# Mixture-of-experts block: gates spread over partitions once a chunk, products weighted six steps later, gate computation placed between steps

## The reference, cut to what matters

```
def _L1_ffn_ref(x, w_gate, w_g, w_u, w_d):      # 8 experts, 2 chosen, 176 hidden units each
    scores = x @ w_gate
    topk_scores, topk_idx = top_k(scores, 2)
    topk_probs = softmax(topk_scores)
    gating = sum(one_hot(topk_idx, 8) * topk_probs[..., None], axis=-2)
    hidden = silu(einsum('bsd,edm->ebsm', x, w_g)) * einsum('bsd,edm->ebsm', x, w_u)
    expert_out = einsum('ebsm,emd->ebsd', hidden, w_d)
    return einsum('bse,ebsd->bsd', gating, expert_out)
...
x = x + 0.5 * _L1_ffn_ref(layernorm(x), ...)    # twice in the program
```

## Time and profile before

| | |
|---|---|
| three timed executions | 3160.64, 3164.51, 3164.62 us; median 3164.51 |
| profiled execution, its own time | 3132.56 us |
| its span, first to last instruction | 3130.8 us |
| PE / DVE / ACT / POOL busy, share of the span | 80 / 82 / 72 / 64 % |
| mean granted PE clock, 1.00 = 2.4 GHz | 0.931 |
| first call of `ffn1`: start, first matmul of step 0, end | 944.3, 962.2, 1170.65 us |
| second call of `ffn1`: the same | 2903.7, 2921.6, 3127.7 us |

### The profile page before, as it was taken

One profiled execution on the slowest core, in us unless ns is written; L12 is line 12 of the kernel. 1 busy time (PEld: TensorE's weight loads), 2 busy tenths in 40 slices (PEclk: granted clock), 3 DMA queues, 4 the chain that ended last, 5 costly groups with the idle time before them and its releaser, 6 DMA issues. The chain is left out here.

```text
span 3130.8 us, 61223 instructions
## 1 busy us (share of the span) xinstructions
PE 2497.2 (80%) x18663; PEld 1032.7 (33%) x18790; DVE 2578.9 (82%) x4251; ACT 2257.5 (72%) x2453; POOL 1995.7 (64%) x1350
## 2 busy tenths in 40 slices
PE   3655999997658984788888888888888888874899
PEld 3632333334654552122222222222222222213455
DVE  4666888885566656899999999999999999977665
ACT  4432777776444543599999999999999999992454
POOL 4510222222634441699999999999999999983444
PEclk9976999998778996799999999999999999995899
DMA  3222100010210002000000000000000000000000
GB/s 114 68 74 71 30 28 29 28 29 8 64 51 1 1 0 88 14 15 12 12 13 14 12 12 14 13 12 12 14 13 12 12 15 12 12 1 1 4 11 14
DMA packets 77234, 74.71 MB, mean 24 GB/s; under 512 B 16112, under 2 KB 57592, under 8 KB 76992
## 3 DMA queue, kind: packets, MB, share of 16 engines
q1 hardware_dynamic: 72832, 64.47, 7.0%
q0 software_dynamic: 4288, 8.82, 0.9%
HBM read 48.04 MB, written 24.42 MB: 23 GB/s over the span
## 5 line engine op out<-in xcount | busy, mean ns | idle before, releaser
L1730 POOL TENSOR_TENSOR a_sg<-a_sg,a_shifted 128x1664 f32<-128x1664 f32 x256 | 955.6, 3733 | 21.4
L1927 DVE TENSOR_REDUCE a_mx<-a_pm 128x1 f32<-128x1024 f32 x512 | 619.4, 1210 | 21.9 <-PE a_pm L1769 21.8
L1936 DVE TENSOR_SCALAR a_sg<-a_pa 128x1024 int32<-128x1024 int32 x512 | 619.2, 1209 | 4.2 <-PE a_pa L1769 3.9
L1849 ACT ACTIVATE a_pt<-a_pb 128x1024 f32<-128x1024 f32 x512 | 523.6, 1023 | 108.4 <-PE a_pb L1769 108.4
L1786 PE MATMUL a_po<-a_pt,a_Vh 128*32 128x512 f32 x2048 | 540.6, 607 | 2.2 <-ACT a_sg L1868 2.2
L1786 PE MATMUL a_po<-a_sg,a_Vh 128*32 128x512 f32 x2048 | 540.6, 607 | 0.0
L1727 POOL TENSOR_SCALAR a_shifted<-a_sg,a_parh 128x1664 f32<-128x1664 f32 x256 | 470.4, 1838 | 101.9 <-DVE a_sg L1936 64.2
L1864 ACT ACTIVATE a_sg<-a_sg,a_parh 128x2048 f32<-128x2048 f32 x256 | 511.9, 2000 | 0.0
L1868 ACT ACTIVATE a_sg<-a_sg 128x2048 f32<-128x2048 f32 x256 | 489.9, 1914 | 0.0
L1769 PE MATMUL a_pm<-all_K,all_Q 96*128 96x512 bf16 x1024 | 316.2, 391 | 149.9 <-DVE a_mx L1927 123.8
L1548 ACT ACTIVATE a_pt<-a_ring 128x1024 f32<-128x1024 f32 (+2 forms) x384 | 313.5, 846 | 167.4 <-PE a_ring L1475 164.1
(11 more groups left out here) (278 smaller groups left out, 4718.6 us busy)
## 6 DMA issues: line engine op xcount, KB each, us to landing
all_Q<-q_parts SPq DMA_DIRECT2D x256, 48.0 KB
all_K<-k_parts SPq DMA_DIRECT2D x256, 48.0 KB
k_parts<-p_parts SPq DMA_DIRECT2D x16, 384.0 KB, 2.8
all_Q<-a_rows SPq DMA_DIRECT2D x384, 2.0 KB
e_recs<-routed_rows SPq DMA_DIRECT2D x70, 64.5 KB, 1.8
n_xn<-expert_rows SPq DMA_DIRECT2D x16, 256.0 KB, 4.9
q_parts<-p_parts SPq DMA_DIRECT2D x16, 192.0 KB, 2.3
q_parts<-p_parts SPq DMA_DIRECT2D x8, 384.0 KB, 2.6
```

The source lines that it names most:

```text
L1730: nc.gpsimd.tensor_tensor(buf[:, :, 0:CUT], buf[:, :, 0:CUT], shifted[:], ALU.mult)\
L1849: nc.scalar.activation(pt[(j - LT) % 4][:, i, :], pb[:], ACT.Exp, scale=SC)\
L1927: nc.vector.tensor_reduce(mx[:, (j // PER) % 2, t:t + 1], pm[:], AX.X, ALU.max)\
L1936: nc.vector.tensor_scalar(sg[(j - LS) % 4][:, i, :].bitcast(I32), pa[:].bitcast(I32), SIGN_OFF, None, ALU.bitwise_and).then_inc(abs_done, 1)
```

## The change

The hidden units are laid out anew: of each tile's 128 partitions, 16 belong to each expert. So one and the same spread of gates over partitions serves all 11 tiles of a chunk. In detail:

- The `sel` matrix, its load, `gateT`, `gate3`, the bf16 identity, the three-way split of the gates, the 32 transposes ahead of the steps and the seventh matmul of every step go.
- POOL makes `wide` (`widen`), the gates of four token tiles with each expert's value repeated 16 times, once a chunk. PE transposes it (`turn`, 4 fp32 transposes a chunk) into `psm`, after step k=5 of the chunk.
- DVE's `products` is split in `product` (`su`) and `weigh` (`hid`). `weigh` for a step is issued six steps later, `high` and `low` seven steps later. `su` grows from 2 to 11 tiles, and PE no longer waits for `hid`.
- The output of a chunk is cut in four pieces, one token tile (33 matmuls) each, issued after steps k=9 of the next chunk and k=1, 4 and 6 of the one after it. `psy` takes two banks used in turn; DVE adds each piece one step later. The last seven pieces come after the last step.
- The gate computation is cut in three parts of DVE's stream, ahead of products 0, 1 and 4 of chunk 0. The Exp moves behind the third silu on ACT.

The diff, cut to its core:

```diff
-    sel = m.sb("sel", [96, KT1, P], BF16)
-        eng.dma_start(sel[:], w["sel"].rearrange("r (k p) -> r k p", p=P)).then_inc(sem, 16)
...
+    LAG = 6
+    TURN = 5
+    PIECES = ((1, 2, 1), (4, 2, 2), (6, 2, 3), (9, 1, 0))
...
+        wide = m.sb("wide", [P, 2, 4, E1, P // E1])
-        psy = m.ps("psy", [P, 4, D])
+        psy = m.ps("psy", [P, 2, CH])
...
-                nc.gpsimd.memset(gate3[:], 0.0).then_inc(cleared, 1)
+                def widen(c, p):
+                    if known(c, 1):
+                        pool.wait_ge(gate_ready, 1)
+                    elif not known(c, 2):
+                        pool.wait_ge(turned, c - 1)
+                    nc.gpsimd.tensor_copy(wide[:, p], gate[:, bass.ds(4 * c, 4), :].unsqueeze(3)
+                                          .broadcast_to([P, 4, E1, P // E1])).then_inc(widened, 1)
...
+                def turn(c, p):
+                    pe.wait_ge(widened, c + 1)
+                    if not known(c, 2):
+                        pe.wait_ge(hid_done, KT1 * (c - 1))
+                    for q in range(4):
+                        last = nc.tensor.transpose(psm[:, p, q * P:(q + 1) * P],
+                                                   wide[:, p, q].rearrange("p e i -> p (e i)"), ident[:])
+                    last.then_inc(turned, 1)
...
                         pe.wait_ge(silu_done, s - 1)
                         pe.wait_ge(su_done, s - 1)
-                        pe.wait_ge(hid_done, s - 1)
...
-                    nc.tensor.matmul(psm[:, b, :], sel[:, k, :], gateT[:, bass.ds(c * CH, CH)],
-                                     start=True, stop=True).then_inc(m_done, 1)
...
+                def output(c, p, q):
+                    if q == 0:
+                        pe.wait_ge(low_done, KT1 * c + KT1)
+                    if not known(4 * c + q, 2):
+                        pe.wait_ge(added, 4 * c + q - (1 if isinstance(c, int) or q != 1 else 0))
+                    for k in range(KT1):
...
+                def body(c, p):
+                    live = not after(c)
+                    for k in range(KT1):
+                        if live:
+                            step(c, p, k)
+                            if k == TURN:
+                                turn(c, p)
+                        for at_k, back, q in PIECES:
+                            if at_k == k and not known(c, back):
+                                if live or back == 2:
+                                    output(c - back, (p + back) % 2, q)
+                    if not live:
+                        for q in range(4):
+                            output(c - 1, 1 - p, q)
...
+                def weigh(c, p, k):
+                    s = KT1 * c + k
+                    if k == 0:
+                        dve.wait_ge(turned, c + 1)
                     dve.wait_ge(su_done, s + 1)
-                    if s_min(s) >= 3:
+                    if not known(s, 3):
                         dve.wait_ge(low_done, s - 2)
-                    nc.vector.tensor_tensor(hid[:, k % 4, :], psm[:, b, :], su[:, b, :], ALU.mult)\
+                    nc.vector.tensor_tensor(hid[:, k % 4, :], psm[:, p, :], su[k], ALU.mult)\
                         .then_inc(hid_done, 1)
...
+                        if known(c, 1):
+                            gates(k)
+                        if live:
+                            product(c, p, k)
+                        then = earlier(c, p, k, LAG)
+                        if then:
+                            weigh(*then)
```

More of the change, by code:

```diff
@@ L760, in ffn1, with slots @@
         psm = m.ps("psm", [P, 2, CH])
-        psy = m.ps("psy", [P, 4, D])
[L762 to L768, removed]
+        psy = m.ps("psy", [P, 2, CH])
+        chain, e2, saved, widened, gate_ready, turned = (
+            m.sem(x) for x in ("chain", "e2", "saved", "widened", "gate", "turned"))
+        g_done, u_done, silu_done, su_done, hid_done, high_done, low_done, y_done, added = (
+            m.sem(x) for x in ("gd", "ud", "silu", "sud", "hidd", "high", "low", "yd", "added"))
+        def slots(eng, body):
             for p in range(2):
@@ L840, in step @@
                         nc.tensor.matmul(out[:, b, :], low, xh, start=False, stop=True).then_inc(done, 1)
-                    nc.tensor.matmul(psm[:, b, :], sel[:, k, :], gateT[:, bass.ds(c * CH, CH)],
-                                     start=True, stop=True).then_inc(m_done, 1)
[L844 to L854, removed]
+                def output(c, p, q):
[4 more added lines that the diff above has]
+                    for k in range(KT1):
+                        high, low = (part[p][:, k, q * P:(q + 1) * P] for part in (hidh, hidl))
+                        nc.tensor.matmul(psy[:, q % 2, 0:D], high, wdh[:, k, :], start=(k == 0), stop=False)
+                        nc.tensor.matmul(psy[:, q % 2, 0:D], high, wdl[:, k, :], start=False, stop=False)
+                        last = nc.tensor.matmul(psy[:, q % 2, 0:D], low, wdh[:, k, :], start=False,
+                                                stop=(k == KT1 - 1))
@@ L855, in output, with body @@
                     last.then_inc(y_done, 1)
-                def chunk(c, p):
+                def body(c, p):
+                    live = not after(c)
                     for k in range(KT1):
[L859 to L864, removed]
+                        if live:
[9 more added lines that the diff above has]
+                            output(c - 1, 1 - p, q)
@@ L866, in _ @@
+                slots(pe, body)
             @block.scalar
             def _(act):
[L868 to L873, removed]
                 def silu(c, p, k):
@@ L891, in chunk @@
                     for k in range(KT1):
[L892 to L899, removed]
+                        if live:
+                            silu(c, p, k)
+                        if known(c, 1) and k == 2:
+                            act.wait_ge(e2, 1)
+                            nc.scalar.activation(pr[:, 1, :], pr[:, 0, :], ACT.Exp).then_inc(e2, 1)
@@ L908, in _ @@
[L908 to L915, removed]
@@ L943, in products @@
                         .then_inc(hid_done, 1)
-                def add(c):
-                    dve.wait_ge(y_done, c + 1)
-                    for q in range(4):
-                        nc.vector.scalar_tensor_tensor(X[:, 4 * c + q, :], psy[:, q, :], 1.0 / WSCALE,
-                                                       X[:, 4 * c + q, :], ALU.mult, ALU.add).then_inc(added, 1)
-                def chunk(c, p):
-                    for k in range(KT1):
-                        products(c, p, k)
-                        if k == EARLY - 1 and not (isinstance(c, int) and c == 0):
-                            add(c - 1)
```

127 lines of the change are left out of this document (71 added, 56 removed).

## The result

| | before | changed |
|---|---|---|
| median of the timed runs | 3162.57 us (3160.55 to 3164.62, 4 runs) | 3089.99 us (3088.97 to 3090.72, 4 runs) |
| ratio | | 0.9781, 95% interval 0.9769 to 0.9793 |
| profiled execution, span | 3132.56, 3130.8 us | 3088.97, 3086.9 us |
| first call of `ffn1`, start to end | 226.3 us | 189.2 us |
| second call | 224.0 us | 189.7 us |

The kernel is 72.6 us faster; 60 were predicted. The two calls, read in one profile of each kernel, account for 37.1 + 34.3 = 71.4 us. The two profiled spans differ by only 43.9 us, because the profiled execution of the kernel before was an unusually quick one ahead of the change's place; the first experiment shows this.

A forecast was written before the change was run, and what follows sets the result against it. PE's matmuls plus a two-step wait for `hid` were taken as the bound; calls change by -31.1 and -28.7 us, the start by -0.5, so 3164.5 - 60.3 = 3104 us, range 3092 to 3113.

The forecast's parts named there:

- the fourteen steps: Step 6 of chunk 0 to step 9 of chunk 1: DVE sets the pace, 1.46 us a step, 20.4 us.
- What bounds the steps: Kernel before: seven matmuls take 1.51 us a step, but waiting for `hid` makes two steps take 3.17 us.
- The front: Before a call's first step: step 0 no longer waits for gates, first matmul from 17.8 to about 0.1 us, -17.7 us.
- The first steps: Chunk 0 up to step 6, at half clock: step 6 starts 14.2 us in; gates between steps cost 3.6 us.
- The table loads: ACT's switches to Exp and back: 1.28 us a load, no drain; with the skill's drain, 5.5 us longer.
- the rival built on it: DVE sets the pace everywhere: a chunk costs 23.9 us, 18 us more in all, 3122; chance 0.13.
- Six chunks at 22.45 us: The six full chunks of a call: PE's stream of 22.05 us plus 0.4 each, 134.7 us.
- handover: Full chunks: 0.05 us added for each of eight changes a chunk between steps, turn and pieces.
- The tail: After a call's last step: PE idles 5.4 us, clock falls, 21.4 us; +7.0 and +9.6 us for the calls.
- At the start: Kernel start: one DMA issue goes from a queue that is waited for, -0.5 us.
- POOL's copies: POOL's 512-element copy, once a chunk: 0.7 us, no cost to DVE; rival that it makes the kernel slower, chance 0.02.
- The profiled execution: Whole kernel: the timed median's 32 us above the profiled execution, not located in the trace, was taken as unchanged.

The follow-up runs named there:

- the first experiment: The unchanged kernel before, profiled once more; one run, 3158.69 us.
- the later wait: Against the kernel before, PE's wait for `hid` of step s-2 moved from ahead of a step's first matmul to ahead of its seventh; 3148.05 us, ratio 0.9959.
- the changed kernel's second profile: The changed kernel run once more, unaltered, on the same chip as the version with the last output summed tile by tile; 3093.02 us, ratio 0.9778.

## Why the prediction was right, and where it was off

The mechanism was the forecast one in every part but the fourteen steps below, and the gain was larger than forecast. The measured 3090 lies 2 us below the forecast's own range of 3092 to 3113, an outcome that had a chance of 0.04. The base accounts for 2 us: the prediction started from 3164.5, and the median beside the result is 3162.6.

- **What bounds the steps.** PE's stream plus a two-step wait for `hid`. Both held: the later wait gave 13 us, and a seventh matmul in each step of the changed kernel cost 34 to 36.
- **The front, -17.7.** Measured -17.8: the first matmul starts with the call.
- **The first steps, 14.2 us to step 6.** Measured 13.0 and 14.4. The two calls differ by when the clock rose, 3.1 and 6.0 us after the first matmul; 4.9 was taken. PE's two pauses are where they were expected, for product 1 and for the copy. The copy was put at 0.7 and took 0.61.
- **The table loads.** Silu 2 ended at 977.43, the load began at 977.44 and Exp 1.29 us later; the next load began 0.02 after Exp's end, and silu 1.29 after that. The drain of about 1.38 us that the Trainium skill adds ("ScalarE: Activation LUTs", "What ACT_TABLE_LOAD costs") does not show. The prediction's estimate from it, 5.5 us more in all, would have made 3110, the worse number.
- **Fourteen steps without outputs, 20.4 us. This step failed.** They took 18.7 and 18.6, at 1.29 to 1.30 a step and 0.5 for the turn of chunk 1. The prediction read DVE's pace as 0.73 us an instruction off rows in which the product's start was set by PE and the weighting's by the product just ahead of it. Ready instructions of this size start 0.60 apart, so DVE needs 1.20 to 1.30 a step and not 1.46, and PE sets the pace here too. With every weighting twice, three instructions took 1.80. The distance of two instructions of which one waits is not the engine's pace. The size was off by 3.5 us over both calls, and the rival built on it was no rival.
- **Six chunks at 22.45 us.** Measured 22.05, PE's sum to the hundredth. The 0.05 us a handover, 4.8 us in all, was an allowance for nothing; the earlier trace rows had shown none.
- **The tail, 21.4 us in both calls.** Measured 20.4 and 19.4, 3 us less. POOL's low parts went at 1.12 us rather than 1.19 and ended 10.0 us after the last step, not 10.9. PE idled 3.67 us and not 5.4, for this reason and because the wait of 0.65 us for an add came before. The clock fell to half in both calls, as taken, but in the second only 3.3 us of output ran at half, against 5.3 in the first, and that call's output took 1.0 us less.
- **At the start, -0.5 us,** is too small to be seen here.
- **Sum.** Start 1, fourteen steps 3.5, handovers 4.8, tail 3.0: these make up the 12 us between 60 and 72. All of them err to the dear side, so nothing cancelled.
- **POOL's copies.** Eight in a call at 0.61 us, and the products and weightings beside them took their usual 0.68 to 0.69. By the Trainium skill ("GPSIMD Engine Reference", "Specifications") POOL contends with DVE instructions in a two-port mode or with two SBUF inputs. These have one input in PSUM, and the trace agrees.
- **The profiled execution.** The prediction carried the 32 us between profile and median along as a constant. That came out right because they lay in stages that the change doesn't touch. Nothing that the prediction had read showed it, so this part was luck; only the second profile shows it.

## What to carry to other kernels

When PE is nearly full, read the distance between starts of equal steps and not its busy time: 3.17 us for two steps whose matmuls need 3.02 named the wait. A matmul that only moves a small operand to the right partitions can cost as much as one that computes; laying the weights out so that all tiles share one spread removed 176 of them, and this was the largest part of the gain in the steps. The adds of a chunk are better spread out than done in one go, where the engine that makes them also feeds PE. A long lag between pipeline stages is paid once at the end, and there the last sum should be ordered by what becomes ready, which here gave back another 12 us. Whether a lag of six steps was needed is not shown: no run has the new layout with a shorter one.

## What the runs showed of the hardware that was not expected

- DVE products of 128x512 with a recorded duration of 0.68 us start 0.60 us apart when their inputs are ready, so durations overlap on DVE too.
- The clock's fall doesn't follow from the length of the pause alone. In the first steps it was at half right behind a pause of 3.51 us. In the tails of the changed kernel and its variants it fell within the last pause (3.67 us) in some calls, and in others only after PE had worked again for 0.9 to 1.4 us, as in the second call of the changed kernel's second profile, below. After a pause of 3.30 us at the same place it fell in one of the four calls of the kernel before, within the pause, and stayed full in three; in the first call of the run with the later wait it fell 1.0 us after PE had resumed.

Windows of that second call (start, end, length, busy by engine, clock, DMA); PE resumes between the first and the second row:

```profile
3076.00:3078.00 2.00, 0.00 (x0) 0.00 (x0) 0.00 (x0) 0.09 (x1) 1.97 (x2) 1.00 0.46 131
3078.00:3080.00 2.00, 1.98 (x31) 1.98 (x32) 0.00 (x0) 0.00 (x0) 0.00 (x0) 0.85 0.00 0
3080.00:3082.00 2.00, 2.00 (x21) 2.00 (x20) 0.29 (x1) 0.00 (x0) 0.00 (x0) 0.50 0.00 0
```
